# A new order of VectorE's work in the groups, and scatters split in fours, in a layer norm, attention and expert kernel

## The chip, the core and the metric

One of the cores of a Trainium2 chip runs the whole program in one launch. The metric is the time of that launch on the device, in microseconds, the median of several runs. A traced execution comes beside it: it shows every instruction of TensorE (PE), VectorE (DVE), ScalarE (ACT), GpSimd (POOL) and the queue of SyncE (SP).

## The reference

The input x is 2 x 2048 tokens of 256 channels, all float32. It is attention with one agent per token, a layer norm, a layer of experts with a shared expert beside them, and a second layer norm:

```python
agent = einsum('bnc,c->bn', q, w_conv1)            # q, k, v from x and w_qkv
agent_attn = softmax(einsum('bn,bnc->bc', agent * scale, k))
agent_v = softmax(einsum('bc,bnc->bn', agent_attn, v))
agent_v = einsum('bn,bnc->bc', agent_v, v)
x = layernorm(x + softmax(agent[:, :, None], -1) * agent_v[:, None, :])

scores = softmax(xf @ gate_w.T)                    # 8 experts, the best 2 of each token
h = einsum('td,ehd->teh', xf, W1); y, g = split(h, 2)
eo = einsum('teh,edh->ted', y * silu(g), W2)
z = einsum('te,ted->td', w_dense, eo) + gated_mlp(xf, Ws1, Ws2)   # hidden 192, shared 384
x = layernorm(x + z)
```

## The kernel before, in words

Every engine has its own program, written out by hand, in the order in which it runs; semaphores join them. The 4096 tokens are 32 tiles of 128 rows, and 8 groups of 4 tiles. Products are made exact by splitting each operand in a high and a low part: ScalarE rounds a piece (`...hi`), another engine subtracts (`...lo`), and TensorE makes three products, high by high, low by high and high by low.

**Start (0 to 45 us).** The attention's sums, and the weights. The weights come in 10 pieces through a ring of three buffers: ScalarE's `high(n)` makes the high part, POOL's `low(n)` (line 546) the low one. Pieces 0 to 5 have their low part made in this stage; pieces 6 to 9 (the second weights of the experts, 128x1024 each) in four instructions of 256 columns each, behind the scatters of groups 1 to 4. The load of a piece waits until the ring buffer's last piece has its low part, and SP's first load of sorted rows waits for all ten (`s_wlo`), as the row buffers lie on the ring.

**Group stage (45 to 165 us), groups 0 to 6.** For group g, TensorE runs: the logits of the router (`logits_of`), the first layer of the shared expert in three pieces (`first_layer(g, 0..2)`), the places (`places`), the second layer in three parts (each waits for `htlo` of its piece, the first also for `product(g, 1)`), and, between the first and the second of these, the transposes of group g + 1. VectorE's program is `group(g)`: `route` (the best two experts), `tables` (where the experts' blocks will lie), `product(g, m)` (hidden times silu), `hidden_lo(g, m)` (the low part of it), `inverse_std(g + 1)` (a Newton step on the root), `slots(g)` (the row of each token in the sorted buffer), `layer_norm(g + 2, tiles)` (the attention's result added to x, with its row sum), `rows_lo(g + 1)` (the low part of the transposed rows) and `add_routed_input(g, u)` (the shared expert's result). ScalarE rounds, makes the silu, normalises group g + 1 (`normalise`, into `x2`, one of two buffers, once the scatters of the group before in that buffer have landed) and sums the squares of group g + 2.

POOL waits for `s_slot`, and then issues 8 indirect transfers for the group (4 tiles, 2 choices; "scatters"), which write the rows of `x2` to the sorted buffer `rows_in` in HBM. Between them, or behind them in group 0, stands `rough_rstd`: a power of -0.5, the rough root of group g + 2, which waits for that group's squares.

**Block stage (165 to 305 us).** The sorted rows are 71 blocks of 128 rows of one expert, worked on in 36 pairs. In step i TensorE transposes pair i + 1, multiplies pair i by `w1`, transposes the products of pair i - 1 and multiplies pair i - 2 by `w2`. SP loads the rows of each block (`load_rows`, line 446). The first 8 pairs hold rows of groups 0 to 2 alone, and are loaded early; the load of pair 8 waits until the second table is there (`s_tbl`), and until all the scatters of all eight groups have landed (line 465); later ones wait for the row buffer. ScalarE scales each result (line 831), and POOL stores it with two indirect transfers a pair (line 654) in the order of the tokens. Group 7's logits and slots are made at this stage's start, so that its 8 scatters (line 596) stand in POOL's queue ahead of the stores of pair 0. Later POOL adds the results to x (`ADDS`) and makes rough roots for the second layer norm (`ROUGH`, ahead of the stores of pairs 21, 27 and 31).

**End (305 to 337 us).** The shared expert of group 7, the last results, and the second layer norm.

The lines of SP that hold back pair 8 are:

```python
            sp.wait_ge(s_tbl, 2)
            rows = rows_of(FULL // 2)
            for n in range(2):
                sp.wait_ge(s_sc[n], 16 * K * G * NP)
            sp.wait_ge(s_pad, 16 * (IDLE + E))
            for j in range(FULL // 2, PAIRS):
                load_rows(j, rows)
```

## Time and profile before

| | |
|---|---|
| time, median of 3 runs | 339.32 us (338.72 to 341.7) |
| the profiled execution's own time | 339.15 us |
| its span, first to last instruction | 337.4 us |
| TensorE busy | 311.0 us, 92% |
| VectorE busy | 266.3 us, 79% |
| ScalarE busy | 194.8 us, 58% |
| POOL busy | 205.2 us, 61% |
| chain that ended last, by engine | PE 54%, DVE 17%, DMA 9%, POOL 8%, ACT 5% |

Busy times are those of the whole span; a matmul's row runs past the start of the next. The granted clock of TensorE has two levels, 1.2 GHz (0.50 in the rows) and 2.4 GHz (1.00). A row of the timeline has a start in us, a duration, the engine, the line, the operation, what it writes and reads, and how often it stands there in a row (x4: four, merged in one). Behind it stands in brackets how long the engine was idle before it, and what ended that.

### The profile page before, as it was taken

The page shows a single profiled execution, that of the slowest core. Times are in us where ns is not written, and L with a number is a line of the kernel's source. Part 1 is how long each engine was busy: PE and PEld are TensorE (multiplying, and loading weights), DVE is VectorE, ACT ScalarE, POOL GpSimd, SP SyncE. Part 2 cuts the span into 40 slices and gives each one's busy share as a digit, 9 for nine tenths or more (in the row PEclk, how much of TensorE's full clock was granted, in tenths as well). Part 3 has the DMA queues.
Part 4 walks back from the last instruction along what each step waited for, and adds up shares of the span by engine and source line. Part 5 has one row for each costly group of instructions (what it writes and reads, how often), then busy time and mean ns, then how long its engine had stood idle before and what let it go on. Part 6 is the DMA issues. An engine that isn't in the chain of part 4 may idle for free.

```text
span 337.4 us, 7796 instructions
## 1 busy us (share of the span) xinstructions
PE 311.0 (92%) x2190; PEld 277.4 (82%) x2190; DVE 266.3 (79%) x1083; ACT 194.8 (58%) x442; POOL 205.2 (61%) x241
## 2 busy tenths in 40 slices
PE   3889799999999999999999999999999999999960
PEld 2456688769798879888889999999999999998850
DVE  2795679865888898885789877776799889998686
ACT  1045686637374646465445666666655588688473
POOL 5049650746768776875757544447576856868760
PEclk9979999899999999999999999999999999999996
DMA  7977420211192111153257544447988988876953
GB/s 227 374 257 258 149 65 0 85 48 65 67 254 70 65 65 67 66 159 119 97 159 249 153 152 131 139 140 166 241 234 218 226 208 198 234 219 182 354 198 124
DMA packets 31383, 54.63 MB, mean 162 GB/s; under 512 B 4880, under 2 KB 22544, under 8 KB 31344
## 3 DMA queue, kind: packets, MB, share of 16 engines
q1 hardware_dynamic: 23136, 29.82, 28.5%
q0 software_dynamic: 8208, 24.32, 25.6%
q8 instruction: 20, 0.33, 0.5%
q14 instruction: 19, 0.16, 0.1%
HBM read 29.73 MB, written 24.40 MB: 160 GB/s over the span
## 4 chain that ended last, share of the span: by engine, by line
PE 54%; DVE 17%; DMA 9%; POOL 8%; ACT 5%; issue 3%; SPq 2%; DVEq 0%; ACTq 0%
PE bank L1129 19%; PE bank L1163 10%; PE bank L1012 8%; POOL rows_in L596 4%; PE bank L1093 4%; DMA stage<-ws_t 4%; PE bank L1036 4%; PE bank L996 3%; DMA x<-rows_out 2%; POOL w1lo L552 2%; PE bank L1143 2%; DVE htlo L1468 2%; DVE xs L1259 2%; DVE mix L1462 2%; DMA rows_in<-x,slot 2%
## 5 line engine op out<-in xcount | busy, mean ns | idle before, releaser
L654 POOL DMA_INDIRECT rows_out<-stage,place x71 | 69.8, 983 | 49.0 <-ACT stage L831 32.5
L596 POOL DMA_INDIRECT rows_in<-x,slot x64 | 64.6, 1009 | 47.0 <-DVE slot L1374 30.5
L1129 PE MATMUL bank<-w1hi,bx 128*128 x284 | 64.0, 346 | 0.2 <-DVE bx L1483 0.2
L1129 PEld LDWEIGHTS bank<-w1hi,bx 128*128 128x128 f32 x284 | 48.3, 188 | 0.7 <-issue 0.7
L811 ACT ACTIVATE stage<-bank 128x384 f32<-128x384 f32 (+1 forms) x36 | 17.5, 487 | 36.6 <-PE bank L1129 36.5
L831 ACT ACTIVATE stage<-bank,weight 128x256 f32<-128x256 f32 x71 | 30.0, 470 | 11.0 <-PE bank L1163 9.5
L1129 PE MATMUL bank<-w1lo,bx 128*128 x142 | 36.3, 336 | 0.0
L1483 DVE TENSOR_TENSOR bx<-bank,bx 128x512 fp32r<-128x512 f32 (+1 forms) x36 | 24.5, 684 | 13.5 <-ACT bx L753 13.1
L1036 PE MATMUL bank<-ws2hi,hthi 128*128 128x256 f32 x96 | 28.7, 299 | 5.0 <-DVE htlo L1468 3.3
L1012 PE MATMUL bank<-xthi,ws1hi 128*128 128x512 f32 x96 | 31.6, 411 | 0.0
L1012 PE MATMUL bank<-xthi,ws1lo 128*128 128x512 f32 x96 | 30.5, 400 | 0.0
L745 ACT ACTIVATE mix<-bank 128x512 f32<-128x512 f32 x24 | 14.1, 589 | 28.3 <-PE bank L1012 28.3
L1012 PE MATMUL bank<-xtlo,ws1hi 128*128 128x512 f32 x96 | 30.3, 398 | 0.0
L749 ACT ACTIVATE hthi<-mix 128x512 fp32r<-128x512 f32 x24 | 15.1, 629 | 20.2 <-DVE mix L1462 20.2
L1036 PE MATMUL bank<-ws2lo,hthi 128*128 128x256 f32 x96 | 26.7, 278 | 0.0
L1036 PE MATMUL bank<-ws2hi,htlo 128*128 128x256 f32 x96 | 26.7, 278 | 0.0
L1129 PEld LDWEIGHTS bank<-w1lo,bx 128*128 128x128 f32 x142 | 25.7, 188 | 0.0
L1036 PEld LDWEIGHTS bank<-ws2hi,hthi 128*128 128x128 f32 x96 | 18.1, 188 | 8.6 <-DVE htlo L1468 6.5
L1199 DVE CUSTOM_DVE_ANT_0 junk<-xs,bank 128x256 f32<-128x256 f32 x64 | 22.8, 415 | 2.9 <-DMA xs<-x 2.6
L1462 DVE TENSOR_TENSOR mix<-bank,mix 128x512 f32<-128x512 f32 x24 | 16.5, 686 | 8.8 <-ACT mix L745 8.6
L1163 PE MATMUL bank<-w2hi,hthi 128*128 x71 | 22.8, 321 | 0.0
L753 ACT ACTIVATE bx<-bank 128x512 fp32r<-128x512 f32 (+1 forms) x36 | 21.2, 591 | 1.9 <-PE bank L1093 1.9
(251 smaller groups left out, 871.9 us busy)
## 6 DMA issues: line engine op xcount, KB each, us to landing
stage<-rows_in SPq DMA_DIRECT2D x71, 133.0 KB, 2.6
xs<-rows_out POOLq DMA_DIRECT2D x12, 512.0 KB, 6.1
xs<-x SPq DMA_DIRECT2D x8, 512.0 KB, 8.3
out<-xs SPq DMA_DIRECT2D x7, 512.0 KB
stage<-w_t SPq DMA_DIRECT2D x8, 384.0 KB, 3.9
rows_in<-clear SPq DMA_DIRECT2D x16, 133.0 KB
rows_out<-stage,place POOLq DMA_INDIRECT x71
stage<-w_t SPq DMA_DIRECT2D x2, 512.0 KB, 3.9
```

Source lines behind the costliest of these rows:

```text
L596: pool.indirect_dma_start(rows_in[0:E * CAP, :], bass.IndirectOffsetOnAxis(slot[:, q * G + t, k:k + 1], 0), x2[q % 2][:, t, :], None).then ...
L654: pool.indirect_dma_start(rows_out[:, :], bass.IndirectOffsetOnAxis(place[:, 2 * j + b:2 * j + b + 1], 0), by[j % 4][:, b * C:(b + 1) * C] ...
L753: act.activation(bxhi[j % 2][:, 0:C * width(j)], bank_x[j % 2][:, 0:C * width(j)], ACT.Copy).then_inc(s_bxhi, 1)
L811: act.activation(bsg[j % 2][:, 0:width(j)], bank_h[j % 2][:, 0:width(j), H:F], ACT.Silu).then_inc(s_bsg, 1)
L831: ins = act.activation(by[j % 4][:, b * C:(b + 1) * C], result(j, b), ACT.Copy, scale=weight[:, j // 2 % 2, at_w:at_w + 1])
L1012: mm = pe.matmul(bank[:], w[:, k, o:o + P], xt[:, k, :], start=(a == 0), stop=(a == len(steps) - 1))
L1036: mm = pe.matmul(bank[:, (t % 2) * C:(t % 2 + 1) * C], ht[:, m, t * P:(t + 1) * P], w[:, m, :], start=(t % 2 == 0 and n == 0 and a == 0), ...
L1129: mm = pe.matmul(bank_h[j % 2][:, b, 0:F], bx[j % 2][:, (2 * b + k) * P:(2 * b + k + 1) * P], w[:, bass.ds(e, 1), k, :], start=(a == 0), s ...
L1163: mm = pe.matmul(result(j, b), ht, w[:, bass.ds(e, 1), :], start=(a == 0), stop=(a == len(steps) - 1))
L1199: vec.tensor_tensor_reduce(junk[:, nth % 2, :], xs[:, tile, :], row, 1.0, 0.0, ALU.mult, ALU.add, dst[:, b, t:t + 1]).then_inc(s_dot, 1)
L1462: vec.tensor_tensor(prod[buf(g, m)], hidden_banks(g, m)[0][:], sg[buf(g, m)], ALU.mult).then_inc(s_pr, 1)
L1483: vec.tensor_tensor(bxlo[j % 2][:, at], bank_x[j % 2][:, at], bxhi[j % 2][:, at].bitcast(F32), ALU.subtract).then_inc(s_bx, 1)
```

## The change

Four things:

- **Low pieces.** Pieces 6 to 9 have their low part made by VectorE (`weights_lo`), in one instruction each: piece 6 in group 1 ahead of `product(1, 1)`, pieces 7, 8 and 9 at the end of groups 2, 4 and 5. POOL keeps pieces 0 to 5.
- **Order in the groups on VectorE.** In group 0, `rows_lo(1)` comes ahead of the token shift and all four layer norm tiles. In group 1, `product(1, 1)` comes ahead of the root (`inverse_std(2)`), and two layer norm tiles go behind `slots`. From group 2 on, `slots` comes ahead of the first two layer norm tiles, and the fourth goes behind the last `hidden_lo`.
- **Scatters.** In every group but the last, the rough root (in group 6 a wait for the shared add) stands between the fourth and the fifth of the 8. Of group 7, four come at once, two behind the stores of pair 0, and two behind those of pair 2.
- **Second norm.** The rough roots of pairs 21, 27 and 31 go from ahead of the pair's two stores to between them.

```diff
             def low(n):
 
                 pool.wait_ge(s_whi, n + 1)
-                size = HI[n].shape[1]
-                width = size if n < 6 else 2 * P
-                for at in (slice(c, c + width) for c in range(0, size, width)):
-                    ins = pool.tensor_tensor(LO[n][:, at], RAW[n][:, at], HI[n][:, at].bitcast(F32), ALU.subtract)
-                ins.then_inc(s_wlo, 1)
+                pool.tensor_tensor(LO[n], RAW[n], HI[n].bitcast(F32), ALU.subtract).then_inc(s_wlo, 1)
...
             for q in range(NG):
                 pool.wait_ge(s_slot, q + 1)
-                for t in range(G):
-                    if t == 2 and 0 < q < NG - 2:
-                        rough_rstd(q + 2)
-                    for k in range(K):
-                        pool.indirect_dma_start(
-                            rows_in[0:E * CAP, :], bass.IndirectOffsetOnAxis(slot[:, q * G + t, k:k + 1], 0),
-                            x2[q % 2][:, t, :], None).then_inc(s_sc[q % 2], 16)
-                if q == 0:
-                    rough_rstd(2)
-                elif q < 5:
-                    low(5 + q)
+                for t in range(2):
+                    scatter(q, t)
+                if q < NG - 2:
+                    rough_rstd(q + 2)
+                elif q < LAST:
+                    pool.wait_ge(s_zev[0], q + 1)
+                if q < LAST:
+                    for t in range(2, G):
+                        scatter(q, t)
...
             for j in range(PAIRS):
                 if j % 2 == 0:
                     pool.wait_ge(s_to, j // 2 + 1)
-                if j in ROUGH:
-                    rough_rstd2(ROUGH[j])
                 if j < BY_BLOCK:
...
+                    if b == 0 and j in ROUGH:
+                        rough_rstd2(ROUGH[j])
+                if j in (0, 2):
+                    scatter(LAST, 2 + j // 2)
...
+            def weights_lo(n):
+
+                vec.wait_ge(s_whi, n + 1)
+                vec.wait_ge(s_wlo, n)
+                vec.tensor_tensor(LO[n], RAW[n], HI[n].bitcast(F32), ALU.subtract).then_inc(s_wlo, 1)
+
+            LOW_AT = [2, 4, 5]
...
                 hidden_lo(g, 0)
                 if g == 1:
+                    weights_lo(6)
+                product(g, 1)
+                if g == 1:
                     inverse_std(2)
                     value_row(1)
-                    layer_norm(after, range(2, G))
-                product(g, 1)
...
-                elif g > 1 and after < NG:
+                slots(g)
+                if g == 1:
+                    layer_norm(after, range(2, G))
+                if g > 1 and after < NG:
                     layer_norm(after, range(0, 2))
-                slots(g)
...
                     hidden_lo(0, 2)
+                    rows_lo(1)
                     token_shift(1)
-                    layer_norm(after, range(0, 2))
+                    layer_norm(after, range(G))
                 if g > 1 and after < NG:
-                    layer_norm(after, range(2, G))
+                    layer_norm(after, range(2, G - 1))
                 if g:
                     hidden_lo(g, 2)
-                rows_lo(g + 1)
-                if g == 0:
-                    layer_norm(after, range(2, G))
+                if g > 1 and after < NG:
+                    layer_norm(after, range(G - 1, G))
+                if g:
+                    rows_lo(g + 1)
                 for u in range(2):
                     add_routed_input(g, u)
+                if g in LOW_AT:
+                    weights_lo(7 + LOW_AT.index(g))
```

`scatter(q, t)` is the old pair of indirect transfers of one tile, as a function.

**POOL, from group 7's scatters to the stores of pair 3.** Before, all eight scatters (`rows_in<-x_1`) stand ahead of the first store (`rows_out<-stage`), the eight in two rows:

```order
L596 DMA rows_in<-x_1,slot 33792x266 [waits slots]
L596 DMA rows_in<-x_1,slot 33792x266 x7
L654 DMA rows_out<-stage,place 17408x256 [waits expert_row,block_places]
L654 DMA rows_out<-stage,place 17408x256
L654 DMA rows_out<-stage,place 17408x256 [waits expert_row]
L654 DMA rows_out<-stage,place 17408x256
L654 DMA rows_out<-stage,place 17408x256 [waits expert_row,block_places]
L654 DMA rows_out<-stage,place 17408x256
```

In the changed kernel (line numbers differ), the same place:

```order
L589 DMA rows_in<-x_1,slot 33792x266 [waits slots]
L589 DMA rows_in<-x_1,slot 33792x266 x3
L653 DMA rows_out<-stage,place 17408x256 [waits expert_row,block_places]
L653 DMA rows_out<-stage,place 17408x256
L589 DMA rows_in<-x_1,slot 33792x266 x2
L653 DMA rows_out<-stage,place 17408x256 [waits expert_row]
L653 DMA rows_out<-stage,place 17408x256
L653 DMA rows_out<-stage,place 17408x256 [waits expert_row,block_places]
L653 DMA rows_out<-stage,place 17408x256
L589 DMA rows_in<-x_1,slot 33792x266 x2
```

Four scatters moved: two behind the first pair's stores, two behind the third pair's.

**VectorE, from group 0's last `hidden_lo` to the next logits.** `htlo` is written by `hidden_lo`, `small` by the token shift, `xs,rowsum` by the layer norm, `xtlo` by `rows_lo`, `xs<-bank` by the adds. Before:

```order
L1468 TENSOR_TENSOR htlo<-mix,hthi 128x512 [waits hidden_hi]
L1241 COPY small<-bank 128x1 [waits att1_tensor]
L1259 SCALAR_TENSOR_TENSOR xs,rowsum<-row,tok,xs 128x256 x2
L1329 TENSOR_TENSOR xtlo<-bank,xthi 128x512 [waits x2t_hi] x2
L1259 SCALAR_TENSOR_TENSOR xs,rowsum<-row,tok,xs 128x256 x2
L1477 TENSOR_TENSOR xs<-bank,x_0 128x512 [waits shared_psum0]
```

Now:

```order
L1471 TENSOR_TENSOR htlo<-mix,hthi 128x512 [waits hidden_hi]
L1332 TENSOR_TENSOR xtlo<-bank,xthi 128x512 [waits x2t_hi] x2
L1244 COPY small<-bank 128x1 [waits att1_tensor]
L1262 SCALAR_TENSOR_TENSOR xs,rowsum<-row,tok,xs 128x256 x4
L1480 TENSOR_TENSOR xs<-bank,x_0 128x512 [waits shared_psum0]
```

`xtlo` comes first, and the four layer norm tiles stand together behind it.

**VectorE, group 2, from `product(2, 1)` to the next logits.** `mix` is written by the products, `slot` by the slots, `w2lo` by the low piece. Before:

```order
L1462 TENSOR_TENSOR mix<-bank,mix 128x512 [waits silu]
L1259 SCALAR_TENSOR_TENSOR xs,rowsum<-att,tok,xs 128x256 [waits value_row1,token_softmax]
L1259 SCALAR_TENSOR_TENSOR xs,rowsum<-att,tok,xs 128x256
L1362 TENSOR_TENSOR slotf<-bank,begin 128x32 [waits positions]
...
L1468 TENSOR_TENSOR htlo<-mix,hthi 128x512 [waits hidden_hi]
L1462 TENSOR_TENSOR mix<-bank,mix 128x512 [waits silu]
L1259 SCALAR_TENSOR_TENSOR xs,rowsum<-att,tok,xs 128x256 x2
L1468 TENSOR_TENSOR htlo<-mix,hthi 128x512 [waits hidden_hi]
L1329 TENSOR_TENSOR xtlo<-bank,xthi 128x512 [waits x2t_hi] x2
L1477 TENSOR_TENSOR xs<-bank,x_0 128x512 [waits shared_psum0]
L1477 TENSOR_TENSOR xs<-bank,x_0 128x512 [waits shared_psum1]
L1336 TENSOR_REDUCE logits<-bank 128x32 [waits logits]
```

Now:

```order
L1465 TENSOR_TENSOR mix<-bank,mix 128x512 [waits silu]
L1365 TENSOR_TENSOR slotf<-bank,begin 128x32 [waits positions]
...
L1471 TENSOR_TENSOR htlo<-mix,hthi 128x512 [waits hidden_hi]
L1465 TENSOR_TENSOR mix<-bank,mix 128x512 [waits silu]
L1262 SCALAR_TENSOR_TENSOR xs,rowsum<-att,tok,xs 128x256
L1471 TENSOR_TENSOR htlo<-mix,hthi 128x512 [waits hidden_hi]
L1262 SCALAR_TENSOR_TENSOR xs,rowsum<-att,tok,xs 128x256
L1332 TENSOR_TENSOR xtlo<-bank,xthi 128x512 [waits x2t_hi] x2
L1480 TENSOR_TENSOR xs<-bank,x_0 128x512 [waits shared_psum0]
L1480 TENSOR_TENSOR xs<-bank,x_0 128x512 [waits shared_psum1]
L1487 TENSOR_TENSOR w2lo<-stage,w2hi 128x1024 [waits weights_lo,weights_hi]
L1339 TENSOR_REDUCE logits<-bank 128x32 [waits logits]
```

The slots moved ahead of two layer norm tiles, one tile moved behind the last `htlo`, and the low piece stands ahead of the next `route`.

## Rows read from the trace of the kernel before

**Rows 1.** Busy time by stage: window, its length, each engine's busy us (instructions), clock, DMA share.

```profile
core 0: us, PE busy (x) PEld busy (x) DVE busy (x) ACT busy (x) POOL busy (x), PEclk, DMA share, GB/s
45.00:165.00 120.00, 116.38 (x756) 99.53 (x756) 95.37 (x390) 67.44 (x154) 74.69 (x85) 0.99 0.28 87
165.00:305.00 140.00, 139.53 (x1002) 136.97 (x1001) 116.92 (x473) 90.48 (x215) 86.95 (x90) 1.00 0.71 191
```

**Rows 2.** Waits of TensorE from 45 to 165 us: total, times, longest.

```profile
PE bank L1036 <- DVE mix L1462: 1.4, 2, 0.9
PE bank L1036 <- DVE htlo L1468: 1.2, 4, 0.4
PE bank L996 <- DVE xtlo L1329: 0.8, 1, 0.8
```

**Rows 3.** Timeline of TensorE, group 1's logits to group 2's second piece.

```profile
61.61 0.36 PE L996 MATMUL bank<-gate,xthi 128*128 128x16 f32 x2 [0.77 <-DVE xtlo L1329]
...
63.38 0.71 PE L1012 MATMUL bank<-xthi,ws1hi 128*128 128x512 f32 x2
...
67.83 1.95 PE L885 MATMUL bank<-xs,stage 128*32 128x256 f32 x32
...
83.81 0.71 PE L1012 MATMUL bank<-xthi,ws1hi 128*128 128x512 f32 x2
...
86.65 0.62 PE L1012 MATMUL bank<-xthi,ws1hi 128*128 128x512 f32 x2
```

**Rows 4.** Two short windows, columns as in the first group; PEclk is third from last.

```profile
64.50:67.90 3.40, 3.40 (x13) 2.19 (x15) 1.96 (x17) 0.11 (x2) 2.63 (x3) 0.50 0.35 125
...
124.50:128.00 3.50, 2.58 (x17) 2.06 (x16) 3.47 (x13) 3.08 (x6) 0.90 (x2) 1.00 0.00 0
```

**Rows 5.** Timeline of TensorE: first layers of groups 3 and 4, longest wait.

```profile
100.27 0.71 PE L1012 MATMUL bank<-xthi,ws1hi 128*128 128x512 f32 x2
...
116.59 0.71 PE L1012 MATMUL bank<-xthi,ws1hi 128*128 128x512 f32 x2
...
126.70 0.36 PE L1036 MATMUL bank<-ws2hi,hthi 128*128 128x256 f32 x1 [0.92 <-DVE mix L1462]
```

**Rows 6.** Timeline of VectorE beside POOL's piece in group 3, and without one.

```profile
88.96 0.66 DVE L1268 TENSOR_TENSOR rn<-vareps,rn 128x4 f32<-128x4 f32 x1
...
104.90 0.16 DVE L1268 TENSOR_TENSOR rn<-vareps,rn 128x4 f32<-128x4 f32 x1
...
107.31 2.08 DVE L1259 SCALAR_TENSOR_TENSOR xs<-att,tok,xs 128x256 f32<-128x256 f32 x1
...
109.33 0.47 DVE L1259 SCALAR_TENSOR_TENSOR xs<-att,tok,xs 128x256 f32<-128x256 f32 x1
...
113.26 1.28 DVE L1329 TENSOR_TENSOR xtlo<-bank,xthi 128x512 fp32r<-128x512 f32 x2
...
106.26 2.85 POOL L552 TENSOR_TENSOR w2lo<-stage,w2hi 128x256 fp32r<-128x256 f32 x4
```

**Rows 7.** Timeline of POOL and ScalarE: group 2's last scatter, and `normalise(4)`.

```profile
105.28 0.96 POOL L596 DMA_INDIRECT rows_in<-x,slot  x1 [0.30 <-issue]
...
108.00 2.08 ACT L733 ACTIVATE x<-xs,minus,rstd 128x256 f32<-128x256 f32 x4 [1.33 <-DMA rows_in<-x,slot]
```

**Rows 8.** Timelines of POOL, SP, TensorE at pair 8; last, the block loads' landing.

```profile
180.18 0.96 POOL L596 DMA_INDIRECT rows_in<-x,slot  x1 [0.30 <-issue]
...
188.42 0.96 POOL L654 DMA_INDIRECT rows_out<-stage,place  x1 [2.21 <-ACT stage L831]
189.69 0.96 POOL L654 DMA_INDIRECT rows_out<-stage,place  x1 [0.30 <-issue]
...
189.29 0.34 SPq L446 DMA_DIRECT2D stage<-rows_in  x1
...
194.68 0.60 PE L1093 MATMUL bank<-ident,stage 128*128 128x128 f32 x4
...
DMA to landing us min/median/max: 2.0/2.6/5.4
```

5 lines of the change are left out of this document (added).

## The prediction

> **What bounds the kernel now.** I read the stages first, then TensorE's waits, then its timeline at each wait, and last the queues of POOL and SP. TensorE is the bound nearly everywhere: it is busy 116.38 of the 120 us of the group stage (45 to 165 us) and 139.53 of the 140 us of the block stage (165 to 305 us) [rows 1]. Work taken off another engine is therefore worth only what TensorE loses by waiting for it. In the group stage the listed waits are 1.4 + 1.2 + 0.8 = 3.4 us [rows 2]. A matmul's row ends later than its place in the pipeline (rows of 0.28 us whose starts lie 0.12 us apart), so each of these seven waits is some 0.15 us longer than listed.
>
> A second loss is the clock. After that wait and the sixteen small matmuls of the logits (16 columns each, 61.61 to 63.38), the granted clock is 0.50 from 64.5 to 67.9 us, the lower of the two levels (1.2 GHz instead of 2.4), and 1.00 before and after [rows 3, 4]. The price can be read off one piece of work: `first_layer(1, 0)` runs from 63.38 to 67.83 = 4.45 us; the same piece in group 2 runs from 83.81 to 86.65 = 2.84 us [rows 3]. So 1.6 us. A wait of 0.92 us at 126.70 us was not followed by the lower clock [rows 4, 5].
>
> The waits of groups 2 to 6 have two sources. POOL's low pieces (four instructions in 2.85 us) run while VectorE makes the root and the layer norm: an operation of 4 elements that takes 0.16 us takes 0.66 us beside a piece, and a layer norm tile 2.08 us instead of 0.47 [rows 6]. And ScalarE's `normalise` waits for scatters: the eighth of group 2 is issued at 105.28 and ScalarE goes on at 108.00, 2.7 us later, after 1.33 us of idling [rows 7].
>
> **The change part by part.**
>
> *Group 0 to 1.* `rows_lo(1)` goes ahead of the token shift and two layer norm tiles. These two (0.47 us each beside their read-out, about 0.9 us together with the shift) are what the logits of group 1 wait for. Moved behind, they cost the logits nothing; but the add of the routed input comes about as late as before (its work ahead is the same), so `first_layer(1, 0)`, which waits for it, gains 0.6 of the 0.77 us. With the wait gone, the small matmuls follow other matmuls directly, as they do in groups 2 to 6, where the listed rows show no lower clock. I count the 1.6 us as gained. Sum 2.2 us; from below 0, if VectorE is late all the same.
>
> *The low pieces.* VectorE gets four operations of 128x1024. The trace has none; two of 128x512 take 1.28 us together [rows 6], so 1.3 us each, 5.2 us in 120, of which VectorE uses 95.37 [rows 1]. Piece 6 lies ahead of `product(1, 1)`, while VectorE waits for TensorE; pieces 7 to 9 lie after the adds, where VectorE waits for the next logits. The cover is about 1 us at each, so `route` starts up to 0.3 us late; TensorE wants its result only behind two pieces of the first layer, 5.7 us of matmuls by the 2.84 us above. I count nothing; if the cover were gone at each of the three, 3 x 1.3 = 3.9 us lost. POOL is rid of 4 x 2.85 us, VectorE of the stretched operations.
>
> *The order in the groups, and the root between the scatters.* Slots come ahead of two layer norm tiles (0.9 us earlier), and in groups 2 to 5 without the 2 us lost to the stretching. The scatters start so much earlier; but the root for the group after next now always stands between the fourth and the fifth, and it waits for that group's squares, which come only at the group's end. From there it is 1.3 us of root, four scatters at 1.27 us spacing and 2.7 us of landing, which reaches `normalise` about when ScalarE comes to it, up to 1 us late in one or two groups. The waits of groups 2 to 6 are the six of the first two rows of [rows 2], 2.6 us as listed and 6 x 0.15 = 0.9 more in truth: 3.5 us, 0.92 us of it in group 4 [rows 5]. I take 2.7 us as gained and leave 0.8 for what the landing leaves. Bounds: nothing, and 3.5 us if all waits go.
>
> Group stage: 2.2 + 2.7 = **4.9 us gained**.
>
> *Group 6's scatters 5 to 8* wait for the shared add at that group's end. Nothing on POOL stands behind them but group 7's scatters, whose slots come only in the block stage. Free.
>
> *Group 7's scatters.* Eight stood in a row, the last at 180.18 us [rows 8]. Now scatters 5 and 6 stand behind the stores of pair 0, and 7 and 8 behind those of pair 2. SP may load pair 8 only when every scatter of every group has landed (line 465, unchanged), and TensorE transposes pair 8 in its fixed order ahead of `w1` of pair 7. In the times of the old trace (both ends move together with the stage, so its gain doesn't matter here):
> - the stores of pair 2 are issued at 188.42 and 189.69, the second done at 190.65; they wait for ScalarE's eviction of that pair, not for the queue;
> - with the spacing of 1.27 us, scatters 7 and 8 are issued at 190.95 and 192.22, and the last lands 2.6 us later, at 194.8;
> - SP then issues the two loads, at 194.9 and, 0.5 us on, 195.5; a load lands in 2.6 us (2.0 to 5.4), so 198.1;
> - TensorE begins these transposes at 194.68, with no wait before it [rows 8].
>
> It will wait 198.1 - 194.7 = **3.4 us**, where in the old trace the loads are issued from 189.29 us and are in time. With the shortest landing it is 2.8 us; one us more is possible with slow landings. Later loads (four pairs ahead) catch up in the queue, SP being free. The block stage has no idle time to give it back in [rows 1], so it goes through to the end. And TensorE stands still four times as long as ahead of the low clock of group 1. I expect the clock to fall once more, at the same price of **1.6 us** (bounds 0 and 3.2 for a second such stretch).
>
> *The roots of the second norm* (pairs 21, 27 and 31) go from ahead of a pair's two stores to between them. The second store starts when it did, the first up to 2 us earlier, and the root waits for no more than before: nothing.
>
> Sum against the profiled execution's own 339.15 us: 339.15 - 4.9 + 3.4 + 1.6 = **339.3 us**. The median of the three runs before is 339.32, so I don't correct for that.
>
> The Trainium skill, "SBUF — State Buffer", section "Who interferes with whom", says that a VectorE instruction with two SBUF inputs and a GpSimd instruction that reads SBUF exclude each other for their whole length, whichever starts second waiting. By that rule, the trace agrees: the stretched rows stand beside POOL's pieces. It speaks against this change too, as the moved pieces have two SBUF inputs and POOL's root reads SBUF.
>
> **The rivals.**
>
> *Faster: the late scatters are hidden.* If pair 2's evictions or the landings left room for the load, only the group stage's gain stayed: 339.15 - 4.9 = 334.3 us. For it: nothing but the uncertainty of my times on two queues. Against: the chain of five steps misses by 3.4 us, and each step has its row.
>
> *The stall, but no low clock:* 339.15 - 4.9 + 3.4 = 337.7 us. For it: the wait at 126.70 left the clock up. Against: that one was 0.92 us.
>
> *Slower: the pieces on VectorE and the root on POOL exclude each other.* The root (1.04 us) comes at the group's end, where pieces 7 to 9 now stand. If a piece waits for a root and then runs 1.3 us, `route` is late by up to 1.3 us, and the product of the next group with it; VectorE has its tables there in groups 3 and 5. Three times 1.3 us takes 3.9 of the gained 4.9: 343.2 us. It decides from about 3.3 us of such loss on (slower by over 1% is over 342.7). For it: the stretched rows. Against: 25 us of free time on VectorE, and the 5.7 us until TensorE wants the result.
>
> **How the numbers follow.** About 1%, 3.4 us, is what a measurement of this kernel can tell from no change. The sum with the stall and the low clock: 0.45, within 1%. The stall alone: 0.22, within 1% for the most part, as 337.7 has 1.9 us to the bound of 335.9; I give 0.04 of it to faster. Hidden scatters: 0.13, faster. The loss on VectorE: 0.13, slower. The rest, 0.07, I divide between the sides (part of the group gain missing with a longer stall; a larger group gain). That makes 0.19 faster, 0.64 within, 0.17 slower. The likeliest case's own range is 337 to 341.5, from a group gain of 3 to 5.7 us and a stall of 2.8 to 4; the range that leaves out 2 in 10 reaches down towards the hidden case and up towards the loss: 335.0 to 342.3 us.
>
> **What would show it.** In the profile after: TensorE's wait for VectorE's `xtlo` at the logits of group 1 gone, and the granted clock 1.00 there; no POOL piece after the first six and no 4-element operation of VectorE over 0.3 us in groups 2 to 5; groups 3 and 4 starting under 16 us apart (now 100.27 to 116.59, 16.32 us [rows 5]); and one wait of TensorE on a load of `rows_in`, some 3 us long, eight pairs into the block stage, with a stretch at 0.50 after it. If that wait is absent or under 1 us, I am wrong to the fast side; if they are still 16.3 us or more apart, the order didn't pay and the time is over 341.

## The result, and the profile after

The changed kernel takes 353.83 us (median of 4 runs, 351.75 to 357.46), the kernel before 340.51 us beside it: a ratio of 1.0386, with a 95% interval of 1.0332 to 1.0441. The ratio leaves out executions over 1.5% above the fastest of their kernel, one on each side here, and so isn't quite the quotient of the medians. The profiled execution took 353.36 us, its span 351.6 us. So the span grew by 14.2 us, where I had forecast no growth.

A table by stage says where they lie. A stage is cut at TensorE's first row of `first_layer` of a group, of the block transposes, and of the last transpose of the tail (`bank<-ident,stage` at 311.76 us before, 324.78 after):

| us | first row of group 0 | groups 0, 1 | groups 2 to 6 | block stage | tail, to TensorE's last row |
|---|---|---|---|---|---|
| before | 46.06 | 37.75 | 80.80 | 147.15 | 15.95 |
| after | 46.91 | 42.13 | 81.75 | 153.99 | 17.34 |
| difference | +0.85 | +4.38 | +0.95 | +6.84 | +1.39 |
| forecast | 0 | -2.2 | -2.7 | +5.0 | 0 |

The 0.85 us ahead of group 0 were not there when both kernels were profiled once more on one chip (45.84 and 45.80), so it is no part of the change. After TensorE's last row the two differ by 0.2 us.

First the page: the granted clock and the DMA share in 40 slices, and the chain that ended last, in which TensorE's share fell from 54% to 37%, while those of POOL and DMA rose from 8 and 9% to 15% each:

```profile
PEclk9989999998999999999999969999999999999987
DMA  7968420283112121217266363445999988886953
...
PE 37%; DMA 15%; POOL 15%; DVE 13%; ACT 11%; issue 6%; SPq 2%; DVEq 0%; ACTq 0%; POOLq 0%
```

TensorE's waits from 45 us on, by what they waited for (us in total, times, longest):

```profile
PE bank L987 <- ACT x L736: 6.7, 4, 5.1
PE bank L1096 <- DMA stage<-rows_in: 4.2, 1, 4.2
PE bank L1039 <- DVE htlo L1471: 4.0, 7, 2.5
PE bank L1146 <- DVE hthi L1636: 0.4, 1, 0.4
```

The kernel before had no such wait over 1.35 us in its trace, and none at the transposes [rows 2]. Three single waits make the first three lines long: one ahead of group 2, one in the block stage, and one of 2.5 us in the tail (e12 below).

**The one ahead of group 2.** SP's rows (the load of piece 9, and the eight "clears", transfers of 133 KB each that fill spare blocks of the sorted buffer), then POOL's last two scatters of group 0, ScalarE's `normalise` and TensorE's transposes:

```profile
70.31 1.25 SPq L425 DMA_DIRECT2D stage<-w_t  x2
71.60 5.00 SPq L430 DMA_DIRECT2D rows_in<-clear  x8
```

```profile
71.42 0.96 POOL L589 DMA_INDIRECT rows_in<-x,slot  x1 [0.30 <-issue]
72.68 0.96 POOL L589 DMA_INDIRECT rows_in<-x,slot  x1 [0.30 <-issue]
...
79.20 2.07 ACT L736 ACTIVATE x<-xs,minus,rstd 128x256 f32<-128x256 f32 x4 [5.73 <-DMA rows_in<-x,slot]
...
81.33 1.97 PE L987 MATMUL bank<-ident,x 128*128 128x128 f32 x8 [5.07 <-ACT x L736]
```

VectorE makes piece 6's low part from 69.06 to 70.28 us. That frees the ring for piece 9, whose load SP issues at once, and behind it the clears: 2 MB beside the scatters of group 0. The last scatter, issued at 72.68, lets `normalise` go on only at 79.20, 6.5 us later; in [rows 7] it was 2.7 us. In the kernel before, POOL made piece 6 some 20 us later, and the clears lay at 93 to 100 us, where no wait for a scatter stands in the trace. Busy time by engine in 3 us stretches, with granted clock, DMA share and GB/s at the end of each row:

```profile
73.00:76.00 3.00, 3.00 (x23) 2.72 (x21) 2.86 (x17) 0.47 (x1) 1.55 (x2) 1.00 1.11 318
76.00:79.00 3.00, 0.26 (x3) 0.06 (x1) 0.62 (x2) 0.00 (x0) 2.09 (x4) 1.00 1.11 256
79.00:82.00 3.00, 0.67 (x3) 0.68 (x4) 0.21 (x1) 2.55 (x5) 0.84 (x1) 0.80 0.91 211
82.00:85.00 3.00, 3.00 (x16) 2.77 (x15) 2.31 (x4) 1.89 (x5) 0.00 (x0) 0.63 0.00 1
```

TensorE does nearly nothing from 76 to 81 us, and has the lower clock from 81 to 84 us: the transposes take 1.97 us instead of 1.09.

**The one in the block stage** is the forecast one:

```profile
198.29 0.96 POOL L589 DMA_INDIRECT rows_in<-x,slot  x1 [0.30 <-issue]
...
201.19 3.61 SPq L446 DMA_DIRECT2D stage<-rows_in  x4
...
205.18 1.11 PE L1096 MATMUL bank<-ident,stage 128*128 128x128 f32 x4 [4.24 <-DMA stage<-rows_in]
```

```profile
205.00:208.40 3.40, 3.22 (x12) 3.22 (x13) 1.38 (x6) 0.60 (x1) 0.00 (x0) 0.50 0.74 185
208.40:211.80 3.40, 3.40 (x20) 3.30 (x19) 1.38 (x6) 1.09 (x2) 0.00 (x0) 0.69 0.37 98
211.80:215.00 3.20, 3.20 (x24) 3.17 (x23) 1.76 (x8) 1.86 (x5) 1.68 (x2) 1.00 0.10 41
```

The next transposes stand at 211.70 and 215.75 us: the round at the lower clock took 6.52 us, the one after it 4.05, so the clock cost 2.5 us.

**The small ones of groups 3, 5 and 6** (0.27, 0.54 and 0.83 us at the transposes). POOL's root and VectorE's low piece of group 2, then `normalise` and TensorE of group 3:

```profile
103.72 1.14 POOL L565 TENSOR_SCALAR vareps<-square 128x4 f32<-128x4 f32 x1 [1.48 <-ACT squares L710]
...
103.59 1.22 DVE L1487 TENSOR_TENSOR w2lo<-stage,w2hi 128x1024 fp32r<-128x1024 f32 x1
...
112.66 2.08 ACT L736 ACTIVATE x<-xs,minus,rstd 128x256 f32<-128x256 f32 x4 [1.87 <-DMA rows_in<-x,slot]
...
114.80 1.09 PE L987 MATMUL bank<-ident,x 128*128 128x128 f32 x8 [0.27 <-ACT x L736]
```

The 4-element `vareps` takes 1.14 us where it meets a low piece (groups 2, 4, 5) and 0.19 us elsewhere.

### The profile page after: what moved, and what is told of

Its sections match the earlier page's. It is cut to its first block, busy times and chain, and to the rows that moved or that the text cites. A ratio compares the mean times of both kernels' runs of the same rounds, so it can differ in the third digit from the quotient of the medians.

```text
span 351.6 us, 7788 instructions
## 1 busy us (share of the span) xinstructions
PE 315.1 (90%) x2190; PEld 282.0 (80%) x2190; DVE 263.1 (75%) x1087; ACT 195.3 (56%) x442; POOL 197.7 (56%) x225
## 4 chain that ended last, share of the span: by engine, by line
PE 37%; DMA 15%; POOL 15%; DVE 13%; ACT 11%; issue 6%; SPq 2%; DVEq 0%; ACTq 0%; POOLq 0%
PE bank L1132 17%; PE bank L1166 9%; POOL rows_in L589 7%; DMA rows_in<-x,slot 6%; PE bank L1096 4%; DMA stage<-ws_t 4%; ACT x L736 4%; ACT squares L710 3%; DVE htlo L1471 3%; DMA x<-rows_out 2%; POOL rough L567 2%; POOL w1lo L549 2%; DVE mix L1465 2%; PE bank L1146 2%; ACT hthi L752 2%
## 5 line engine op out<-in xcount | busy, mean ns | idle before, releaser
L589 POOL DMA_INDIRECT rows_in<-x,slot x64 | 65.4, 1022 | 43.8 <-DVE slot L1377 24.5
L1132 PE MATMUL bank<-w1hi,bx 128*128 x284 | 65.3, 352 | 0.0
L1132 PEld LDWEIGHTS bank<-w1hi,bx 128*128 128x128 f32 x284 | 49.4, 192 | 0.5 <-issue 0.2
L1039 PE MATMUL bank<-ws2lo,hthi 128*128 128x256 f32 x96 | 27.5, 286 | 0.0
L1471 DVE TENSOR_TENSOR htlo<-mix,hthi 128x512 fp32r<-128x512 f32 x24 | 16.6, 692 | 13.9 <-ACT hthi L752 13.8
L1096 PE MATMUL bank<-ident,stage 128*128 128x128 f32 x142 | 21.8, 277 | 4.2 <-DMA stage<-rows_in 4.2
```

What stands on the lines that cost most here:

```text
L589: pool.indirect_dma_start(rows_in[0:E * CAP, :], bass.IndirectOffsetOnAxis(slot[:, q * G + t, k:k + 1], 0), x2[q % 2][:, t, :], None).then ...
L1039: mm = pe.matmul(bank[:, (t % 2) * C:(t % 2 + 1) * C], ht[:, m, t * P:(t + 1) * P], w[:, m, :], start=(t % 2 == 0 and n == 0 and a == 0), ...
L1096: mm = pe.transpose(bank_x[j % 2][:, (2 * b + k) * P:(2 * b + k + 1) * P], xq[j // 2 % 2][:, (2 * j + b) % 4, k * P:(k + 1) * P], ident[:])
L1132: mm = pe.matmul(bank_h[j % 2][:, b, 0:F], bx[j % 2][:, (2 * b + k) * P:(2 * b + k + 1) * P], w[:, bass.ds(e, 1), k, :], start=(a == 0), s ...
L1471: vec.tensor_tensor(htlo[:, c, :], prod[buf(g, m)], hthi[:, c, :].bitcast(F32), ALU.subtract).then_inc(s_ht, 1)
```

## The experiments

Theory after these traces: (a) the early burst of piece 9 and the clears costs 5 us and more ahead of group 2; (b) the late scatters of group 7 cost 4.2 + 2.5 us; (c) the rest of groups 2 to 6 is lost by the low pieces beside POOL's root. Rivals: the losses follow from the root between the scatters; or the scatters are slow of themselves.

The chips differ. On those of e1 to e4, of e14 and e15, and of e16 and e17 the kernel before took 353 to 356 us, on the others 339 to 341. Ratios are always to the kernel before on the same chip; across chips I compare stages. The stages are read from one trace of each run; two traces of one kernel differ by up to 1.1 us in groups 2 to 6 (e9 and e17) and 1.6 in the tail (the changed kernel).

**e1: group 7's scatters ahead of the stores.**

```diff
-                if q < LAST:
-                    for t in range(2, G):
-                        scatter(q, t)
+                for t in range(2, G):
+                    scatter(q, t)
...
-                if j in (0, 2):
-                    scatter(LAST, 2 + j // 2)
```

> The changed kernel, with one part undone: group 7's eight scatters stand in a row again, ahead of every store. In the changed kernel TensorE waits 4.24 us at the transposes of the eighth pair, and the clock then stands at 0.50 for 6.8 us. Theory (the late scatters hold SP's load, the stall brings the low clock): both vanish, the block stage takes 147 us again instead of 154, so 6.8 us less than the changed kernel's 353.8: 347.0 us (346 to 348). Rival 1 (the stall alone is the scatters' doing, the low clock would come anyway in this stage): 4.2 us less, 349.6. Rival 2 (the load is late for a reason in front of it, since the whole stage starts 6 us later): no change, 353.8.

**e2: load and clears held**, and **e3: only the clears held** (the same line, ahead of the clears):

```diff
                 room_for(8 + n)
+                if n == 1:
+                    sp.wait_ge(s_sc[0], 16 * K * G)
```

> The changed kernel, with one wait added on SP: the load of the last weight piece (1 MB) and the eight clears behind it (1.06 MB) start only when group 0's eight scatters have landed. In the changed kernel they are issued from 70.3 to 76.6 us, the last scatter of group 0, issued at 72.7, lands at 79.2, and TensorE waits 5.07 us at 81.3 and has a lower clock for 3.4 us. Theory (the freed ring let SP start a burst that the scatters share the DMA engines with): the scatter lands in under 3.5 us, TensorE's wait shrinks to about 1 us, the low clock stays out: 4 to 5.6 us less than the changed kernel, 349.0 us. Rival 1 (the scatter is slow of itself, two of 2.0 us and a DVE piece beside them): the wait stays, 353.8. Rival 2 (the burst is put off and meets group 1's scatters instead, as the clears did in the kernel before at 93 to 100 us, without a wait there): as the theory for the first, nothing lost later.

> The changed kernel, with the same wait on SP one step later: only the eight clears (1.06 MB, issued from 71.6 to 76.6 us) are held until group 0's scatters have landed; the load of the last piece starts at 70.3 as before. It tells which half of the burst delays the scatter. If the clears do: as the run that holds both, about 349.0 us. If the weight load does (two transfers of 512 KB, ahead of the scatter by 1 to 2 us): the scatter lands by 78 or later and most of the 5.07 us wait stays, 352.5 to 353.8. If both share it by their bytes: a wait of 2 to 3 us, some 351 us.

Kernel before 356.37 us; e1 355.12, e2 354.51, e3 355.70, none told apart from it (ratios 0.9978, 0.9968, 0.9996, each +-0.004). None is near its forecast (347.0, 349.0, and 349 to 353.8), which counted on a chip where the kernel before takes 340 us. As whole times these decide nothing: the block stage took 157.3, 159.7 and 161.0 us here, with the late scatters or without. Near its start ScalarE, VectorE and TensorE stand still for 8.1, 4.8 and 3.6 us, overlapping, while SP issues clears and POOL its scatters; e1's ScalarE:

```profile
188.40 0.49 ACT L811 ACTIVATE stage<-bank 128x384 f32<-128x384 f32 x1 [8.12 <-PE bank L1129]
```

The matmuls named had ended long before. I don't know the cause; it covers (b). The group stage is undisturbed, and there (a) is decided. Groups 0 and 1 take 42.30 us in e1 (as changed), 39.36 in e3, 36.75 in e2; TensorE's wait is 4.38, 2.04 and 1.14 us:

```profile
75.76 1.25 SPq L427 DMA_DIRECT2D stage<-w_t  x2
77.06 5.05 SPq L432 DMA_DIRECT2D rows_in<-clear  x8
...
73.17 0.96 POOL L591 DMA_INDIRECT rows_in<-x,slot  x1 [0.30 <-issue]
...
75.75 2.08 ACT L738 ACTIVATE x<-xs,minus,rstd 128x256 f32<-128x256 f32 x4 [1.81 <-DMA rows_in<-x,slot]
```

Held (e2), the scatter of 73.17 lands in 2.6 us. By these three traces the clears make 2.9 of the 5.5 us, the load 2.6. The put-off burst delays nothing visible. "DMA: Bandwidth & Descriptors" of the Trainium skill, section "SWDGE vs HWDGE vs iDMA", says that inside each DMA engine GpSimd's and SP's transfers sit in different queues, between which the engine goes round. That fits; the runs show only the lateness.

**e4: the root behind all eight scatters.**

```diff
-                if q < NG - 2:
-                    rough_rstd(q + 2)
...
                         scatter(q, t)
+                if q < NG - 2:
+                    rough_rstd(q + 2)
```

> The changed kernel, with POOL's root for the group after next behind all eight scatters of a group instead of between the fourth and the fifth. In the changed kernel POOL idles 1.5 to 7.6 us ahead of the root for the group's squares while scatters 5 to 8 stand behind it. Theory (this wait holds the scatters, which hold ScalarE's normalise for 1.9 to 2.4 us in every second group): the idling stays but holds nothing; TensorE's waits of 0.3 to 0.8 us at the transposes of groups 3, 5 and 7 and at the second layer go: 2.5 to 4 us less, 350.5 us. In group 0 the scatters go 1 us or more earlier, past the burst: up to 5 us less on top, 346. Rival (VectorE's low piece and the root, which exclude each other, cost it): they still meet at the group's end, and the time stays within 1 us of 353.8.

374.9 us, 1.0453 (1.037 to 1.0537) of the kernel before; by far the worst (the traced execution took 377.1 us). Both my theory and the rival fell. The clue is in VectorE's adds of the routed input at the end of group 1:

```profile
84.81 0.96 POOL L589 DMA_INDIRECT rows_in<-x,slot  x1 [0.30 <-issue]
85.84 0.19 POOL L565 TENSOR_SCALAR vareps<-square 128x4 f32<-128x4 f32 x1
86.11 1.04 POOL L567 TENSOR_TENSOR rough<-vareps,half 128x4 f32<-128x4 f32 x1
```

```profile
85.96 0.69 DVE L1480 TENSOR_TENSOR xs<-bank,x 128x512 f32<-128x512 f32 x1 [5.41 <-remote]
87.42 0.69 DVE L1480 TENSOR_TENSOR xs<-bank,x 128x512 f32<-128x512 f32 x1 [0.77 <-remote]
...
86.80 1.19 PE L1015 MATMUL bank<-xthi,ws1hi 128*128 128x512 f32 x2 [3.68 <-DVE xs L1480]
```

The add waits 5.4 us, though the second layer that it needs ended at 81.4 us, and goes on as POOL's row of scatters ends; the second as the root ends. TensorE lost 12.3 us in five such waits. If the two exclude each other, the root between the scatters, where POOL waits for squares, is also the pause in which the adds get through. That is argued from these rows and not shown: the trace names no releaser, and no other run tests it.

**e5: (a) and (b) both undone** (e1's and e2's edits together). **e6: low pieces 6 to 9 on POOL**, behind the scatters of groups 1 to 4. The changed kernel and the one before ran beside them on the same chip.

> The changed kernel with both of the two large suspects undone: group 7's scatters in a row ahead of the stores, and the load of the last weight piece and the clears held until group 0's scatters have landed. Numbers against the changed kernel itself on the same chip, since chips differ. Theory (the two add up: 4.24 us wait and 2.6 us of low clock in the block stage, 5.07 us wait and 1.6 us of low clock ahead of group 2, some 1 us of it not given back): 11 to 13 us less, which is the time of the kernel before or 1 us more. Rival (a late start of the stage is made up elsewhere, so that the two don't add): 7 us less, like one alone.

```diff
+                if 1 <= q <= 4:
+                    low(5 + q)
...
-                if g == 1:
-                    weights_lo(6)
...
-                if g in LOW_AT:
-                    weights_lo(7 + LOW_AT.index(g))
```

> The changed kernel with pieces 6 to 9's low parts back on POOL, behind the eight scatters of groups 1 to 4; the order of the rest as changed. Theory (piece 6's early low part is what lets SP start its burst beside group 0's scatters): group 2's first layer starts 5 us earlier, the burst lies at 90 to 100 us. For groups 2 to 6: theory A (VectorE's pieces beside POOL's root cost the late normalise): no 1.14 us vareps, and no wait of 0.3 to 0.8 us at the transposes; theory B (the root's wait for the squares between the scatters costs it): those waits stay, and POOL's pieces of 2.85 us stretch VectorE's layer norm again, 1 us a group more. Against the changed kernel on the same chip: 6 to 7 us less by A, 3 to 5 us less by B, none if the burst isn't what delays group 0's last scatter.

> The changed kernel itself, as the measure for the two others of this call and for the first four, on a chip where the kernel before took 356 us. If the chip's own cause (instruction reads, slower transfers) only adds to both: 13 us above the kernel before. If it stands at the same places as the changed kernel's waits and covers them: less than 5 us above it.

> The kernel before, for its trace on this chip. On the chip of the first traces it took 339.2 us with no wait of TensorE over 1.4 us from the second stage on. If the chip adds waits for issue in the block stage (as the run with the last scatters first shows, 0.72 us at 186 us and a standstill of 3.6 us behind it), they stand here too.

| us | median | ratio (95%) | groups 0, 1 | groups 2 to 6 | block stage | tail |
|---|---|---|---|---|---|---|
| before again | 339.98 | 1.0013 | 37.79 | 80.88 | 147.36 | 16.22 |
| after again | 352.95 | 1.0405 (1.0354 to 1.0456) | 41.80 | 81.60 | 152.69 | 18.97 |
| e5 | 341.42 | 1.0048 (1.0008 to 1.0088) | 36.73 | 82.40 | 146.86 | 16.78 |
| e6 | 345.17 | 1.0182 (1.0129 to 1.0236) | 35.77 | 80.64 | 152.49 | 17.27 |

e5 is 11.5 us under the changed kernel, in the expected 11 to 13: (a) and (b) add up and are nearly all of the loss. e6 is 7.8 us under it: 6.0 in groups 0 and 1, 1.0 in groups 2 to 6. Its `vareps` rows are all at 0.19 us and TensorE has no wait at the transposes, as theory A says. The stretching that B counts on is there (POOL's pieces take 3.35 us) and costs less.

**e7: the second norm's roots ahead of the stores again**, on top of e5. **e8: pieces 7 to 9 in mid-group**, on top of e5. **e9: the best of both**: e6 with e1's and e7's edits. **e10: e1's kernel** on another chip.

```diff
+                if j in ROUGH:
+                    rough_rstd2(ROUGH[j])
                 if j < BY_BLOCK:
...
-                    if b == 0 and j in ROUGH:
-                        rough_rstd2(ROUGH[j])
```

> The kernel with both suspects undone (341.4 us where the kernel before took 340.0), with one thing more undone: the roots of the second norm (pairs 21, 27 and 31) stand ahead of the pair's two stores again. In the changed kernel the last of POOL's 512 KB loads is issued 0.94 us later against the stage's end than before, VectorE waits 2.03 us for such a load instead of 0.17, and TensorE's wait in the tail is 3.15 us instead of 1.64; with both suspects undone 2.20. Theory (the root between the stores delays the second store, that the load, that the adds): the wait goes back to about 1.6, 0.6 us less, 340.8. Rival (the tail's wait follows from how the landings fall, not from the root): 2.2 us stay, 341.4.

```diff
                 if g == 1:
                     weights_lo(6)
+                if g in LOW_AT:
+                    weights_lo(7 + LOW_AT.index(g))
                 product(g, 1)
```

> The kernel with both suspects undone, and pieces 7 to 9's low parts moved on VectorE from the end of groups 2, 4 and 5 to ahead of the second product, where piece 6's stands. At the group's end they ran beside POOL's root: its first instruction took 1.14 us there and 0.19 us in the other groups. Theory (that exclusion makes the root, the scatters 5 to 8 behind it and ScalarE's normalise late): all vareps rows at 0.19 us, ScalarE's waits of 1.9 to 2.1 us for rows_in down to 1 us, TensorE's waits of 0.3 to 0.5 us at the transposes gone, 1 to 1.5 us less: 340.1. Rival (the root's own wait for the squares, 2 to 3.7 us with scatters behind it, is what counts): waits as they were, 341.4. Second rival (in mid group the piece holds VectorE up ahead of the product): a wait of TensorE for mix or htlo some 0.5 us longer in groups 2, 4 and 5, 342.5.

> What is left of the change when all that lost time is undone: low pieces 6 to 9 on POOL as before, group 7's scatters in a row ahead of the stores, the second norm's roots ahead of the stores; kept are the new order of group 0 (low rows ahead of the token shift and the norm tiles), the slots ahead of the norm, the second product ahead of its root and the root between the scatters. In the run with the pieces on POOL the group stage took 116.41 us against 118.67 before and 123.40 with the change. Theory: that gain of 2.3 us goes through to the end, block stage and tail as before: 337.7 us where the kernel before takes 340.0, faster by 0.7%. Rival (given back in the block stage or the tail): 339.5 to 340.

> The changed kernel with group 7's eight scatters in a row ahead of the stores and nothing else undone: the first run's kernel once more, since that one ran on a chip on which the kernel before took 356 us. Theory (3.66 us of wait and 1.7 us of low clock in the block stage, 5.3 us in all on the second chip; and the tail's wait below 3 us without the clock's fall, 1.2 us more): 352.95 - 6.5 = 346.5. Rival (only the block stage): 347.6. Rival 2 (nothing, as the medians of the other chip seem to say): 353.

| us, before 339.18 | median | ratio (95%) | groups 0, 1 | groups 2 to 6 | block stage | tail |
|---|---|---|---|---|---|---|
| e7 | 341.15 | 1.0053 (1.0019 to 1.0087) | 36.70 | 82.61 | 147.06 | 16.63 |
| e8 | 339.10 | 1.0009 (0.9978 to 1.0041) | 36.71 | 79.36 | 147.61 | 16.87 |
| e9 | 337.86 | 0.9960 (0.9931 to 0.9990) | 35.67 | 80.74 | 147.47 | 15.33 |
| e10 | 345.70 | 1.0163 (1.0098 to 1.0229) | 42.87 | 81.55 | 146.91 | 17.30 |

e8 decides (c). The same pieces on the same engine, a few us earlier in the group, and groups 2 to 6 are 3.0 us shorter than in e5 and 3.2 than in e7, which has e5's group stage and ran on e8's chip. All of it lies in groups 3 to 6 (group 2 takes 15.92 us in e5 and e8), and TensorE's waits at the transposes of groups 3, 5 and 6 (0.32, 0.47, 0.39 us in e5) are gone. The median is 2.0 us under e7's, where I had expected 1 to 1.5; the first row is e5's root, the other two e8's, with ScalarE of group 3:

```profile
99.33 1.14 POOL L567 TENSOR_SCALAR vareps<-square 128x4 f32<-128x4 f32 x1 [2.01 <-ACT squares L709]
```

```profile
98.46 0.19 POOL L567 TENSOR_SCALAR vareps<-square 128x4 f32<-128x4 f32 x1 [1.49 <-ACT squares L709]
...
106.44 2.08 ACT L735 ACTIVATE x<-xs,minus,rstd 128x256 f32<-128x256 f32 x4 [0.91 <-DMA rows_in<-x,slot]
```

"SBUF — State Buffer" of the Trainium skill, section "Who interferes with whom", has the rule (a VectorE instruction with two SBUF inputs and a GpSimd instruction that reads SBUF exclude each other); the trace agrees, 0.95 us at each meeting. Three meetings, 2.85 us on POOL in all, became 3.0 us of the group stage. e10 shows (b) alone: 7.3 us under the changed kernel's 352.95, across two chips of nearly one speed; its block stage is the kernel before's again, and it came 0.8 us under its forecast. e9 came to its forecast (337.7). e7 is within noise of e5 as a whole, and its tail only 0.15 us shorter, which left the tail open.

**e11: what paid, together** (e9, with pieces 7 to 9 as in e8). **e12: only the second norm's roots ahead**, in the changed kernel. Before: 340.82 us.

```diff
-                if 1 <= q <= 4:
-                    low(5 + q)
+                if q == 1:
+                    low(6)
```

> The parts that paid, put together: the run that kept the new order of the groups with every low piece on POOL (337.9 us), with pieces 7 to 9's low parts moved to VectorE ahead of the second product of groups 2, 4 and 5, and piece 6's left on POOL behind group 1's scatters, so that the weight load and the clears stay out of group 0's scatters. In the traces groups 2 to 6 took 80.74 us with the pieces on POOL and 79.36 us with them there on VectorE, 80.88 us before. Theory (the gains of the two places add): groups 2 to 6 in 79.4 us, groups 0 and 1 in 35.7, so 1.3 us less than 337.9: 336.5 us where the kernel before takes 339.2 to 340, faster by 0.8 to 1.2%. Rival (the earlier start meets other waits, or piece 6 on POOL stretches VectorE in group 2 beside piece 7): 337.9 or more.

> The changed kernel with one part undone: the roots of the second norm stand ahead of their pair's stores again; late scatters, early burst and pieces at the group's end stay. Theory (the root between the stores makes the last 512 KB load and so the adds late): the last of POOL's loads is issued 0.9 us earlier against the start of the tail, TensorE's wait in the tail is 1.6 to 2.0 us instead of 3.15, the low clock behind it stays out, and the tail takes 16.5 us instead of 18.97: 2 us less than the changed kernel, 351. Rival (the tail is long because the whole block stage runs late against nothing else, or by chance of the landings): wait above 2.5 us and 353.

e11: 340.79 us, 1.0009 (0.9975 to 1.0042). The gain isn't there: groups 2 to 6 take 82.18 us instead of the expected 79.4, group 2 alone 18.41. VectorE and TensorE in group 2:

```profile
90.63 1.23 DVE L1490 TENSOR_TENSOR w2lo<-stage,w2hi 128x1024 fp32r<-128x1024 f32 x1 [1.41 <-POOL w2lo L552]
```

```profile
92.60 0.35 PE L1042 MATMUL bank<-ws2hi,hthi 128*128 128x256 f32 x1 [2.13 <-DVE mix L1468]
```

VectorE's piece 7 waits for POOL's piece 6 with the product behind it, a wait that my expectation named only in passing.

e12: 351.43 us, 1.0305 (1.0242 to 1.0368), against 1.0405 (1.0354 to 1.0456) for the changed kernel on another chip: 1% less, though the intervals touch. Its tail takes 15.30 us. POOL's last load of `xs`, VectorE and TensorE in the tail, first of the changed kernel (second trace), then of e12:

```profile
318.57 1.01 POOL L611 DMA_DIRECT2D xs<-rows_out  x1
...
325.38 0.75 DVE L1669 BATCH_NORM_STATS2 bst<-xs 128x6 f32<-128x256 f32 x2 [2.03 <-DMA xs<-rows_out]
...
334.15 0.55 PE L1039 MATMUL bank<-ws2hi,hthi 128*128 128x256 f32 x1 [3.15 <-DVE htlo L1471]
```

```profile
319.56 1.00 POOL L611 DMA_DIRECT2D xs<-rows_out  x1
...
333.67 0.36 PE L1039 MATMUL bank<-ws2hi,hthi 128*128 128x256 f32 x1 [0.77 <-DVE htlo L1471]
```

The tails start at 321.89 and 323.79, so the load is issued 3.3 us ahead of its start with the root between the stores and 4.2 ahead without. This holds in every trace: the load is issued 3.3 to 4.0 us ahead of the tail with the root between, 4.2 to 4.7 with it ahead. Nine traces with the root between (e4 left out) have tails of 16.40 to 18.97 us (mean 17.1), ten with it ahead 15.30 to 16.63 (mean 15.9): 1.2 us.

Part of that is the granted clock. Its mean over the tail was 0.90 and 0.82 in the two traces of the changed kernel, 0.90 in e6, and 1.00 in the other six; with the root ahead it was 0.90 in e7 and 1.00 elsewhere. So e7's small gain is partly hidden by the lower clock. At 1.00 throughout, the means are 16.8 and 15.9 us. By these means the late load is worth 0.9 us, and the lower clock lengthened the changed kernel's tail further.

**e14: pieces 7 to 9 in groups 3, 4, 5** (`LOW_AT = [3, 4, 5]` in e11). **e15: two pieces each** (6, 7 on POOL; 8, 9 in groups 4, 5). **e16, e17:** e14's and e9's kernels again, side by side.

> The last combination with piece 7's low part one group later: pieces 7 to 9 on VectorE ahead of the second product of groups 3, 4 and 5. In the last combination piece 7's stood in group 2 and waited 1.41 us there for POOL's piece 6 (the pieces are counted in order), and TensorE waited 2.13 us for the mix at 92.6 us. Theory (that wait between the two engines is all that was lost): TensorE's wait at 92.6 us is gone, group 2 takes 16.2 us instead of 18.41, groups 2 to 6 80 us: 2 us less than the last combination, 0.6% under the kernel before. Rival (group 3 has VectorE's tables, and the piece adds to them): 1 us or more comes back in group 3, and the time is within 1 us of the kernel before.

> As the other kernel of this call, but with pieces 6 and 7 on POOL behind the scatters of groups 1 and 2, and only 8 and 9 on VectorE, ahead of the second product of groups 4 and 5: no piece of VectorE's waits for one of POOL's, and none stands in a group with the full tables. Theory: groups 2 and 3 as in the run with all pieces on POOL (16.27 and 16.47 us), groups 4 to 6 as in the last combination (16.5, 16.9, 14.1): groups 2 to 6 in 80.2 us, some 0.5 us less than with all on POOL, 0.5 to 0.6% under the kernel before. Rival (no gain over all on POOL): 0.4% under the kernel before.

> The kernel with pieces 7 to 9 on VectorE in groups 3 to 5 once more: its first run was on a chip on which the kernel before took 354 us, its groups 2 to 6 took 79.97 us there against 80.88 before (on another chip), groups 0 and 1 35.68 against 37.79. Theory (3.0 us of the group stage gained, block stage as before at 147.4 us, tail as before or 0.6 us shorter): 336.5 us where the kernel before takes 339 to 341, 1% under it. Rival (the 0.8 us against the kernel with every piece on POOL don't reach the end): 337.9, as that one.

> The kernel with every low piece 6 to 9 on POOL and the gains kept, beside the other of this call on one chip: 0.4% under the kernel before, as in its first run, and 0.8 us or 0.2% above the other.

e14: 347.59 us, e15: 348.85, before: 354.17 (0.983, 0.9781 to 0.9879; 0.9843, 0.9794 to 0.9891). e16: 348.82, e17: 350.83, before: 353.39 (0.987, 0.982 to 0.9921; 0.9908, 0.987 to 0.9946). The wait at 92.6 us is gone (group 2: 16.28 us instead of 18.41), and groups 2 to 6 take 79.97 and 80.62 us (e15: 80.49; e17: 81.83). e17's group 3 ran at a clock of 0.90. So the kernels of e14 and e9 were faster than the kernel before on both of their chips, by 0.4 to 1.7%, e9's by 0.4% where the kernel before takes 339 us. That e14's is the faster of the two isn't shown: on the chip that had both, the intervals overlap. How much e14 gains on a 339 us chip wasn't run, and these chips' standstills in the block stage (157 to 160 us here too) may make part of their ratios.

## Why the prediction was wrong

Forecast 339.3 us, range 335.0 to 342.3; it became 353.8. The step that failed is the low pieces' "I count nothing": they cost 6 us in groups 0 and 1 and 3 us in groups 2 to 6. Two smaller terms failed with it, the order's 2.7 us and the "nothing" of the second norm's roots.

- **Group 0 to 1: right.** The wait and the low clock at group 1's logits are gone. With piece 6 out of the way (e6, e9) groups 0 and 1 take 35.7 us instead of 37.8: 2.1 us, forecast 2.2.
- **The low pieces: "I count nothing" was wrong.** I asked what covers 1.3 us on VectorE and not what the finished piece releases. Piece 6 done 20 us earlier gave SP a free ring: 5.1 us (41.80 against 36.73 in e5). It has a second price of 1.0 us (36.73 against 35.77). The scatter beside it takes 2.01 us instead of 0.97, so group 0's last scatter is issued 9.3 us into group 1 instead of 8.2, and TensorE waits 1.14 us at the transposes (e5), where it doesn't in e9. Pieces 7 to 9 cost 3.0 us at the group's end beyond mid-group (e5, e8). My slower rival had the exclusion and nearly the size (3.9), with a wrong path: `route` starts only 0.14 us later behind the logits in e5 than in e8. POOL's root is late, and with it scatters 5 to 8, `normalise`, and TensorE.
- **The order in groups 2 to 6: "I take 2.7 us as gained" was mis-sized.** Alone (e6, e9) it is worth 0.1 to 0.2 us; with the pieces in mid-group 1.5 (e8). I had put all six listed waits down to POOL's pieces and late scatters. Five remain in e9, 0.31 to 0.36 us four times and 0.70 once. The four are waits for `htlo`, the way from product to low part over ScalarE, which the change doesn't shorten; the fifth is for the product of group 4, as before. The late scatters, ahead of `normalise`, held TensorE nowhere in the kernel before: [rows 2] have no wait at the transposes.
- **Group 6's scatters behind the add: free**, as said.
- **Group 7's scatters: right**, in each link. Moved by the 6.3 us between the two traces (TensorE ready at 200.94 instead of 194.68), my times were 198.5 for the last scatter and 201.2 for the load; the rows have 198.29 and 201.19. The wait was 4.24, 3.66, 3.82 and 3.88 us in four traces (forecast 3.4); in the first the load landed 0.8 us later than forecast. The clock cost 2.5 us in that trace, forecast 1.6; the whole block stage grew by 4.9 to 6.8 us, forecast 5.0.
- **The second norm's roots: "nothing" was wrong**, 0.9 us, and 1.2 with what the clock added. I had the second store start when it did, and nothing behind it; the 512 KB load there is issued 0.9 us later against the tail.

Of my signs, the interval of groups 3 and 4 (under 16 us) told it: it was 17.12 us. Against the forecast for each stage, 6.6 us were missed in groups 0 and 1, 3.7 in groups 2 to 6, 1.8 in the blocks, 1.4 in the tail, 0.9 ahead of group 0. The last is no part of the change.

## What to carry to other kernels

When a piece of work is done earlier, follow its signal: who waits for it, what transfer does that start, and whose landing is on the path at that time. Work moved to an idle engine can still hold up another: find what it runs beside at each place in the loop. The same three instructions cost 3 us more at a group's end, beside POOL's root, than in its middle. A gain that rests on waits must name for each wait what chain makes it, or it counts waits that stay.

## What the runs showed of the hardware

- A scatter's landing went from 2.6 to 6.5 us beside 2 MB that SP had issued in 6 us (DMA share 1.11); with the burst held it was 2.6 us again (e2).
- Around TensorE's waits of 2.5 to 5.1 us in the changed kernel (5.07, 4.24 and 2.53 us in the first trace, 3.66 and 3.15 in the second) the granted clock fell to 0.50 for 3 to 7 us. It stayed at 1.00 around waits of 1.14 us (e2), 2.20 (e5, tail) and 2.73 (e10, tail), but fell after 1.79 us in e7's tail. The length of the wait alone doesn't tell.
- VectorE's add of a PSUM bank and an SBUF tile stood 5.41 us beside a row of POOL's scatters (e4), while `xtlo`, of the same kinds of inputs, had run from 79.27 us beside them. Not explained.
- Three of the six chips of the experiments were 4 to 5% slower for the same kernel. In the traces from them ScalarE stood still for 6 to 8 us near the start of the block stage, VectorE and TensorE for 3 to 5 us. Not explained.
